# Decoder kernel, narrow attention: the first scores from keys masked by head, one product of 308 columns per row group in place of four of 77

## The reference, cut to what matters

```python
# x: (64, 128, 128), ctx_512: (64, 77, 64)
def _L1_xattn_ref(q, k, v, Wq, bq, Wk, bk, Wv, bv, Wo, bo):
    HEADS = 16
    D_K = D_MODEL // HEADS            # 128 // 16 = 8
    qh = (q @ Wq + bq).reshape(B, LQ, HEADS, D_K).transpose(0, 2, 1, 3)
    kh = (k @ Wk + bk).reshape(B, LKV, HEADS, D_K).transpose(0, 2, 1, 3)
    vh = (v @ Wv + bv).reshape(B, LKV, HEADS, D_K).transpose(0, 2, 1, 3)
    scores = jnp.einsum('bhqd,bhkd->bhqk', qh, kh) * scale
    attn = jax.nn.softmax(scores, axis=-1)
    out = jnp.einsum('bhqk,bhkd->bhqd', attn, vh)
    return out.transpose(0, 2, 1, 3).reshape(B, LQ, D_MODEL) @ Wo + bo
x = _layernorm(x + _L1_xattn_ref(x, ctx_512, ctx_512, ...), axis=-1)
```

## Time and profile before

| what | value |
|---|---|
| median of the runs | 3613.51 us (3613.43, 3613.51, 3620.50) |
| the profiled execution | 3641.26 us, span 3639.2 us |
| granted TensorE clock, mean over the span | 0.967 |
| narrow attention | about 2936 to 3408 us of the span |
| a group of four batches in its middle | 27.3 us |

### The profile page before, as it was taken

The page is one execution under the profiler, slowest core; times in us unless marked ns, Lnnn a source line. Parts: engine busy times, 40 slices in busy tenths (PEclk is TensorE's granted clock), DMA queues, the critical chain, the costliest instruction groups (busy, mean ns, idle before and its releaser), DMA issues. The chain is left out here.

```text
span 3639.2 us, 102549 instructions
## 1 busy us (share of the span) xinstructions
PE 3335.4 (92%) x41429; PEld 2128.2 (58%) x41429; DVE 2377.2 (65%) x5650; ACT 1971.6 (54%) x3558; POOL 2014.8 (55%) x1778
## 2 busy tenths in 40 slices
PE   7999999998899999898999999999999899999686
PEld 3554555444455555565666666665556567777475
DVE  5888888885555555485565556677777745554465
ACT  5666666663466666442655654336666545555354
POOL 4777877785578787573111115447777712222365
PEclk9999999999999999998999999999999989999798
DMA  4222222224800000000000000000000000000263
GB/s 142 93 82 88 82 92 83 86 80 136 283 2 2 2 2 2 16 1 12 5 5 5 5 3 6 8 8 2 2 2 2 2 21 21 22 15 12 82 178 117
DMA packets 50283, 164.69 MB, mean 45 GB/s; under 512 B 11823, under 2 KB 23218, under 8 KB 40785
## 3 DMA queue, kind: packets, MB, share of 16 engines
q1 hardware_dynamic: 45520, 150.43, 12.4%
q0 software_dynamic: 4352, 8.47, 0.7%
HBM read 149.89 MB, written 43.65 MB: 53 GB/s over the span
## 5 line engine op out<-in xcount | busy, mean ns | idle before, releaser
L504 DVE TENSOR_TENSOR_SCAN XC<-ssm_dA,ssm_db 128x2048 f32<-128x2048 f32 x128 | 565.5, 4418 | 106.5 <-PE ssm_db L359 96.4
L567 POOL TENSOR_TENSOR XC<-XC,XB 128x1536 f32<-128x1536 f32 x128 | 505.7, 3951 | 179.2 <-DVE XC L504 132.3
L373 PE MATMUL ssm_y<-XC,weights 128*128 128x512 f32 x1024 | 472.2, 604 | 2.5 <-POOL XC L567 2.3
L453 ACT ACTIVATE ssm_dA<-ssm_delta,ssm_nega 128x508 f32<-128x508 f32 x512 | 325.1, 708 | 84.1 <-DVE XC L504 83.6
L1193 POOL TENSOR_TENSOR self_pm<-self_pT,weights 128x512 f32<-128x512 f32 x256 | 322.8, 1296 | 64.1 <-ACT self_pT L922 62.7
L373 PEld LDWEIGHTS ssm_y<-XC,weights 128*128 128x128 f32 x1024 | 187.6, 191 | 215.5 <-issue 204.1
L1199 POOL TENSOR_TENSOR XC<-XC,XB 128x128 f32<-128x128 f32 x128 | 58.7, 459 | 399.4 <-DVE XB L1076 399.4
L1624 DVE TENSOR_REDUCE narrow_nmax<-narrow_scores 128x4 f32<-128x308 f32 x256 | 105.0, 472 | 177.5 <-PE narrow_scores L1394 177.4
L1062 DVE TENSOR_REDUCE self_nmax<-self_scores 128x4 f32<-128x512 f32 x256 | 158.5, 682 | 88.2 <-PE self_scores L802 88.2
L2608 POOL TENSOR_TENSOR XC<-XC,weights 128x512 f32<-128x512 f32 x128 | 161.7, 1284 | 95.3 <-ACT XC L2442 95.3
L359 PEld LDWEIGHTS ssm_db<-XB,ssm_dxT 32*128 32x128 f32 x4096 | 135.1, 188 | 99.3 <-DVE XC L504 65.0
(11 more groups left out here) (447 smaller groups left out, 8260.4 us busy)
## 6 DMA issues: line engine op xcount, KB each, us to landing
XB<-c_rows SPq DMA_DIRECT2D x64, 1024.0 KB
sorted<-in_padding SPq DMA_DIRECT2D x1, 33280.0 KB, 110.9
experts_we<-in_w_experts SPq DMA_DIRECT2D x72, 323.0 KB, 2.9
experts_rt<-sorted SPq DMA_DIRECT2D x72, 65.0 KB
ssm_xT<-in_xT SPq DMA_DIRECT2D x16, 256.0 KB
XC<-in_w_experts SPq DMA_DIRECT2D x9, 256.0 KB
weights<-in_w_self SPq DMA_DIRECT2D x1, 1412.0 KB, 7.5
cross_ctx_t<-in_ctx SPq DMA_DIRECT2D x16, 77.0 KB
```

Of the source, the lines that this page charges most:

```text
L373: mm = pe.matmul(yp[half][:, :].rearrange("p (b t) -> p b t", b=GROUP), ident, of_state(states(32, at), k), start=(k == 0 and nq == 0 and ...
L453: o = act.activation(dA[:, p % 2, :].rearrange("p (b k t) -> p b k t", b=GROUP, k=4)[:, :, k, 1:T], by_batch(delta[:, slot, half, :])[:, : ...
L504: dve.tensor_tensor_scan(states(0, p).rearrange("p m t -> p (m t)"), dA[:, p % 2, :], db[:, :], 0.0, ALU.mult, ALU.add).then_inc(h_ready, 1)
L567: pool.tensor_tensor(states(32, p).rearrange("p (b k) t -> p b k t", k=4)[:, :, 0:3, :], states(0, p).rearrange("p (b k) t -> p b k t", k= ...
```

## The change

The queries are no longer masked for the first scores. ACT makes one more copy of them, `qa`, with the plain scale and an unmasked bias (`bias_all`, one more DVE instruction in the set-up). In their place the keys are masked: POOL multiplies the keys of a batch with `own_head`, for the four j side by side, into `km` (128x308 a batch), which lies in the spare part of the buffer `XB`. `first_scores` then has one product per row group, with 32x128 weights from `qa` and 308 columns of `km`. `qm` stays, since `second_scores` uses it. `first_scores(n)` waits for `own_keys`, the semaphore of the key products. On POOL the products of the next group stand between the first and the second scatter of a group.

```diff
-    N_ACT = 6
+    N_ACT = 7
-    SET = 9
+    SET = 10
+        qa = ph.sb("qa", [P, 2, GT])
+        bias_all = ph.sb("bias_all", [P, 1])
+        spare = env["XB"][:, :, :].rearrange("p n t -> p (n t)")[:, RING * GROUP * W:RING * GROUP * W + 8 * GROUP * TK]
+        km = spare.rearrange("p (s b j t) -> p s b j t", s=2, b=GROUP, j=4)
+        own_keys = ph.sem("own_keys")
...
             def context(g):
                 pe.wait_ge(ctx_in[g % 2], 16 * (g // 2) + 16)
-                pe.wait_ge(by_act, g * N_ACT + 5)
+                pe.wait_ge(by_act, g * N_ACT + 6)
...
                 if b == 0:
                     pe.wait_ge(by_act, (n // GROUP + 1) * N_ACT)
+                pe.wait_ge(own_keys, n + 1)
...
-                    for j in range(4):
-                        for r in (2 * two, 2 * two + 1):
-                            rows = slice(32 * r, 32 * r + 32)
-                            mm = pe.matmul(sc[r][:, j * TK:(j + 1) * TK], qm[rows, s, j, b * T:(b + 1) * T],
-                                           kT[rows, s, b * TK:(b + 1) * TK])
+                    for r in (2 * two, 2 * two + 1):
+                        rows = slice(32 * r, 32 * r + 32)
+                        mm = pe.matmul(sc[r][:, 0:4 * TK].rearrange("p (j t) -> p j t", j=4), qa[rows, s, b * T:(b + 1) * T],
+                                       km[rows, s, b])
                     mm.then_inc(s1_mm, 1)
...
+                act.activation(qa[:, g % 2, :], pj[1][:, :], ACT.Identity, bias=bias_all[:, :], scale=SCALE).then_inc(by_act, 1)
...
+            dve.tensor_scalar(bias_all[:, :], V("bq"), SCALE, None, ALU.mult).then_inc(setup, 1)
...
-            def scatter(g):
+            def keys_of_heads(g):
+                pool.wait_ge(by_act, (g + 1) * N_ACT)
+                if g >= 2:
+                    pool.wait_ge(s1_mm, 2 * (g - 1) * GROUP)
+                for b in range(GROUP):
+                    pool.tensor_tensor(km[:, g % 2, b], bcast(kT[:, g % 2, b * TK:(b + 1) * TK], 1, 4), bcast(own_head, 2, TK),
+                                       ALU.mult).then_inc(own_keys, 1)
+
+            def scatter(g, batches):
...
-                for b in range(GROUP):
+                for b in batches:
...
+            keys_of_heads(0)
             for g in range(NG + 3):
                 if g < NG:
                     residual(g)
                 if 0 <= g - 2 < NG:
                     inv(g - 2)
                 if g >= 3:
-                    scatter(g - 3)
+                    scatter(g - 3, (0,))
+                if g + 1 < NG:
+                    keys_of_heads(g + 1)
+                if g >= 3:
+                    scatter(g - 3, (1, 2, 3))
```

## The result

The changed kernel takes 3587.14 us in the median of four runs (3584.10 to 3591.92), the kernel before beside it 3614.23 (3613.43 to 3620.50). These medians are 27 us apart, a ratio of 0.9925; the ratio on record, made from all the runs, is 0.9916, with a 95% interval from 0.9903 to 0.9928. Repeated beside the last experiments it took 3589.60 against 3619.76, ratio 0.9916 again [0.9898, 0.9934]: 30 us less. The forecast's sum was 3586.5. The total came out; several terms of the sum did not, and the rest of this text is about which.

A forecast was written before the change was run, and what follows sets the result against it. PE's work and DVE's maxima were taken as nearly level, the maxima binding after the change. Eleven groups gain 21 us, other beats 4 and 4, start-up loses 1.6: together 27 off the median, 3586.5 us, range 3562 to 3608.

The forecast's parts named there:

- The two chains: PE's own work and DVE's maxima both lead to L1420; the maxima win, so L1420 comes 0.34 us earlier, not 0.61.
- The first rival: The maxima don't bind, so PE's whole 0.61 us a beat counts: about 48 us, 3565 us; chance 0.08.
- the slower one: POOL's key products hold DVE's L141: at 1.34 us each a group gains nothing, at 1.7 some 3628 us; chance 0.08.
- kinds 0 to 3: Narrow-attention beats by t mod 4, four a group; forecast gains 0.34, 0.30, 1.6 and -0.3 us.
- kind 2's 1.6 us: Moving the second scatter away from the first removes the lateness in kind 2: 1.6 of 1.71 us, in eleven groups.
- the 27.8 us: Profiled execution above the median of runs; taken as added by profiling to both kernels, so 27 us came off the median.
- the lateness: In kind 2, beside two POOL scatters, DVE starts its maxima 2.61 us into the beat, not 1.23; 1.4 us a group.
- Kind 3's -0.3: In kind 3 a shorter second half gains 0.3 us; DVE held by key products and moved scatters cost 0.6.
- The start-up: `qa` (0.7 us) and the first key product (0.85) stand before the first scores with PE idle: 1.6 us lost.
- The clock: PE's lower clock level, feared with more idle PE: ten further us at half clock cost 5; widens the range.
- The rival that a less busy PE would run slower: PE, about 95% busy in place of 98%, spends more time at its lower clock and eats the gain; chance 0.05.
- The second rival: The lateness stays in kind 2 or moves whole to kind 3: only 8 to 13 us gained, 3603 us; chance 0.2.

The follow-up runs named there:

- e4: Changed kernel with maxima over only 38 of the 77 keys: 3561.38 us, ratio 0.9841.
- e5: Kernel before with maxima over only 38 of the 77 keys, on the second chip: 3632.55 us, ratio 0.9935.
- e1: Kernel before, unchanged, profiled once more: 3617.51 us, ratio 0.9998; profiled execution 3623.16 us.
- e6: Changed kernel with paired maxima, two reductions of 616 columns in place of four of 308, on the second chip: 3588.68 us, ratio 0.9820.
- e7: Changed kernel with two first-score products of 154 columns per row group in place of one of 308, on the second chip: 3597.39 us, ratio 0.9836.
- e8: Changed kernel with each key product made twice on POOL, one after the other: 3623.21 us, ratio 1.0007.
- e2: Changed kernel with the first scores in their old form; `qa`, key products and moved scatters kept: 3620.67 us, ratio 1.0010.
- e11: Repeat of e2 (changed kernel with the old first scores) in the third series: 3618.71 us against 3619.76, ratio 1.0007.
- e10: Changed kernel, unchanged, timed again in the third series: 3589.60 us.
- e12: Changed kernel with scatters 0 and 1 in a row ahead of the key products, third series: 3590.03 us, ratio 0.9926.
- e9: Kernel before with a fifth reduction a batch on DVE, ahead of the four, into an unread tile: 3715.63 us, ratio 1.0171.

## Why the prediction was right, and where not

**The two chains** held. The first half ready at F+0.90 and L1420 at F+2.79 are what the timeline after shows; e4 shows that the maxima bind, e5 that before the change PE's chain (F+3.00) stood only 0.13 behind them. The first rival (PE's whole saving counts) is out. What was wrong in it did no harm: `weighted` starts at F+0.73 where I reckoned 0.95, and PE's chain could have L1425 at F+2.16 or earlier (e4), not only at 2.52. The first scores' total is 65.6 us where 50 to 60 was forecast. Two of the rivals' sums are off by a little, and nothing hangs on them: the first rival's terms give 46 us where it says 48, and the slower one at 1.7 us gives some 3623, not 3628.

**The beats.** Between e1 and the changed kernel they gain 0.34, 0.33, 0.34 and 0.32 us for kinds 0 to 3: in kinds 0 to 2 one number, the 0.33 by which the first half lands earlier (F+1.23 to F+0.90). In kind 3 the maxima end well before L1425, and the 0.32 is the shorter second half, as forecast (0.3). The forecast had 0.34, 0.30, 1.6 and, with DVE's lateness, -0.3.

**The step that failed is kind 2's 1.6 us,** 18 of the 27 us in the sum. It was read off one profiled execution and subtracted from the median of runs that, by their time, didn't have it. The sentence that the 27.8 us between the profiled run (3641.3) and the median are something "which the profiled state adds to both kernels" is refuted: the profiled execution of the changed kernel is 3584.10, among its timed ones. In e1, at 3623.2, the lateness is gone. Of the 18 us between e1's and the first profile, 11 groups of 1.4 us of lateness make 15. The early groups had made me take the scatters for the whole cause; e1 has the scatters and no lateness.

Where the lateness is there, the 1.6 holds: on the second chip the beat of kind 2 lasts 5.37 us in e6 and 5.49 in e7, against 6.99 in the first profile, 1.6 and 1.5 less. The term was right for that profile and wrong for the runs that it was taken off. Two rows of the first profile, in the beat of the earlier trace rows, show that DVE is not alone in being late:

```profile
3229.61 0.28 ACT L1546 ACTIVATE narrow_rinv<-narrow_sums 128x128 f32<-128x128 f32 x1 [1.27 <-PE narrow_sums L1431]
...
3231.03 1.10 PE L1443 MATMUL narrow_out<-narrow_pT,narrow_v 77*32 77x128 f32 x28 [0.29 <-issue]
```

ACT's wait for PE ends at F+1.00 in place of F+0.13, and PE itself stops for 0.29 us after the first 4 of the 32 records of `weighted`, with no wait that the profile shows. So the lateness looks to lie with PE, on which both wait, and not with DVE; it comes beside POOL's indirect DMAs, and the mechanism stays open.

**Kind 3's -0.3 failed the other way,** by 0.6 us a group. A key product takes 0.69 us, not 0.85, and the four start at F+1.25, so only the last still runs when the L141 come. The forecast had the keys out at F+2.02 from the earlier trace rows; but that row was late itself. In e1 and in the changed kernel they are out at F+1.16, and in e6, on the chip with the lateness, the products start at F+2.09. One L141 of four is held (maximum 808 ns, median 335), as is the small copy L1659 (0.64, where e1, which has no key products, shows 0.16). `add` ends at F+0.99 of kind 3, 0.44 before `weighted` needs it. The mechanism that I priced is real, and e8 shows what the margin was: at 1.4 us of products per batch nothing of the gain is left. "At p = 1.34 a group gains nothing", the recorded rival says; the time agrees, though part of that loss is clock and not beats. The Trainium skill (SBUF — State Buffer, Who interferes with whom) names copy, cast and tensor_scalar as instructions that can block against GpSimd and, on trn2, tensor_reduce as one that can't. The rows agree: in e8 the cast takes 0.69 us and the tensor_scalar 0.83, and in the changed kernel the four reductions of kind 2, from 3197.18 to 3198.81, take 1.63 as ever, with the key products running since 3197.53. The cast touches none of POOL's tiles, so a shared tile isn't the reason.

**The start-up** lost what was reckoned and a little more: 0.67 us of PE's wait for `qa` and 2.0 for the first key products (the group of L1399 above), 2.7 in all. Of these 0.6 stood there before, as the wait for the keys (the row of L1394 in the earlier trace rows), so the loss is 2.1 in place of 1.6.

**The clock,** left out of the sum and feared as a loss, is a gain. 64 beats of 0.33 less 2.1 make 19 us of the 27 to 30 measured. In the third series the mean granted clock of the runs was 0.9671 before and 0.9703 after: 2 x (0.0329 x 3618 - 0.0297 x 3588) = 25 us less at the lower level, worth at most 12. That fits the missing 8 to 11 us. The profiles agree on the chips without the lateness: the middle of the phase is at 0.97, 0.98 and 0.99 in e1, e2 and e11, which have the old product, and at 1.00 in the changed kernel, e10 and e12. (The first profile, with the lateness, has 1.00 as well.) The clock's share is argued from these sums; no run shows it alone. The rival that a less busy PE would run slower did not come true for this change: in the middle PE is busy 100% of the time in e1 and 97% after, and its clock rose. But e9, busy 97% too, has 0.81 there, and e8 0.94: added waiting on DVE did bring stretches at the lower level. Why just these do isn't shown, and I leave it open.

So the total was right by luck, because errors cancelled: of the 27 us, 14 fall away in kind 2 (0.34 in place of 1.6, eleven times) and 2 in the start-up and the other beats; 7 come back in kind 3 and 8 to 11, it seems, from the clock.

The second rival (lateness stays) can't be judged on the chips where there is none. On the second chip e6 and e7 have 0.2 us of it on DVE in place of 1.4, so it mostly goes there. ACT's lateness beside the first scatter is the same in the old form (F+1.00) and the new (F+0.97 and F+0.99), which speaks for the order: the change of form didn't touch that part, and DVE's larger part went when no second scatter followed. That is argued and not shown, since e11 and e12, which would part order from form, met no such chip.

## What to carry to other kernels

A gain in one engine's work counts only up to the next chain: move the shared landing point (here the first half of the scores, 0.33 us earlier) and each beat gains that, no more. An odd wait seen in one profiled execution must be checked against the time of that execution and the median before it enters a sum: 27.8 us above the median was the sign that it was not in the runs. What hangs on the same execution is off with it, here the start of the key products. Work put on an idle POOL is free only as long as the DVE copies, casts and tensor_scalars that it holds have time to spare: 0.7 us a product left 0.44, and 1.4 us left none.

## What the runs showed of the hardware

- The same program takes 3618, 3652 and 3620 us on three chips. The slower one shows, in both kernels of the old form profiled there (e5, e9), DVE starting 1.4 us late beside two indirect DMAs of POOL; a profile of the kernel before on another chip (e1) has the same two DMAs and no such delay. Beside a single one, ACT's wait for a PE result ended at F+0.97 and F+0.99 (e6, e7) in place of F+0.13, and DVE's 0.2 us late.
- A fifth reduction of 0.40 us a beat (e9) brought some 14 us at 1.2 GHz in nine of eleven groups of about 34 us, and cost 64 us in place of 26.
- A float32 tensor_tensor of 128x308 on POOL, one operand broadcast along its innermost dimension and the other along its middle one, takes 0.69 us, below the line between 128x128 (0.46) and 128x512 (1.28), which gives 0.85 us: no price of the broadcast shows.
- For the same columns, 32 records of 32x77 took 1.64 us, 16 of 32x154 took 0.82 (e7), and 8 of 32x308 took 0.80.
- POOL's products started 0.66 us apart. DVE's 0.34 us tensor_scalars beside them took 0.74 to 0.86: held for about one product each.
